# One ScalarE Silu in place of Tanh, Identity and a VectorE join in the feed-forward stage of a transformer layer

## The reference, cut to what matters

```
x = layernorm(x + attention(x))
h = layernorm(x) * ln_gamma + ln_beta
y = silu(h @ w1 + fc1_bias)            # 256 -> 1024, silu(t) = t * sigmoid(t)
z = y @ w2 + fc2_bias                  # 1024 -> 256
x = layernorm(x + (x + 0.5 * z))
```

## Time and profile before

| | |
|---|---|
| median of three runs | 4122.21 us |
| profiled execution | 4118.34 us, span 4116.5 us |
| granted TensorE clock, mean | 0.974 of full speed |
| TensorE busy | 3901.7 us (95%) |
| VectorE busy | 3559.5 us (86%) |
| ScalarE busy | 2781.8 us (68%) |
| GpSimd busy | 867.2 us (21%) |
| last stage | from about 3065 us to the end |

### The profile page before, as it was taken

How to read it: one execution, slowest core, us unless ns; L and a number is a source line. 1 busy time by engine, 2 the same in 40 slices (tenths; PEclk the granted TensorE clock), 3 DMA queues, 4 the chain that set the end, 5 groups by cost and what they waited for, 6 DMA issues and landing times. The chain is left out here.

```text
span 4116.5 us, 78021 instructions
## 1 busy us (share of the span) xinstructions
PE 3901.7 (95%) x22952; PEld 2042.5 (50%) x22952; DVE 3559.5 (86%) x4373; ACT 2781.8 (68%) x5283; POOL 867.2 (21%) x535
## 2 busy tenths in 40 slices
PE   7988999999999999999999999999968999899898
PEld 5653333333333333333333333333326887778777
DVE  6658999999999999999999999999948999989996
ACT  3436888888888888888888888888744444444444
POOL 5430000000000000000000000000006777767774
PEclk9998999999999999999999999999978999999999
DMA  7992113004113211311411311221121122122210
GB/s 253 338 307 55 33 34 82 30 29 82 32 32 64 52 30 41 71 32 32 83 32 32 64 45 32 53 62 32 36 65 53 62 67 76 62 61 68 75 61 26
DMA packets 217885, 286.39 MB, mean 70 GB/s; under 512 B 25521, under 2 KB 127921, under 8 KB 217778
## 3 DMA queue, kind: packets, MB, share of 16 engines
q1 hardware_dynamic: 217778, 285.33, 24.7%
HBM read 165.69 MB, written 118.49 MB: 69 GB/s over the span
## 5 line engine op out<-in xcount | busy, mean ns | idle before, releaser
L685 DVE TENSOR_REDUCE half_max<-first_ps 128x2 f32<-128x1024 f32 x2048 | 2413.4, 1221 | 262.6 <-PE first_ps L579 258.6
L660 ACT ACTIVATE probs<-score_ps 128x512 f32<-128x512 f32 x4096 | 2114.8, 603 | 561.5 <-PE score_ps L604 561.5
L604 PE MATMUL score_ps<-q_s,k_s 49*128 49x512 f32 x4096 | 1435.1, 474 | 22.8 <-DMA q_s<-max_row 7.0
L604 PEld LDWEIGHTS score_ps<-q_s,k_s 49*128 49x128 f32 x4096 | 569.6, 184 | 1279.5 <-ACT probs L660 1179.3
L614 PE MATMUL pv_ps<-probs,v_s 128*32 128x512 f32 x8192 | 1094.2, 606 | 0.0
L579 PE MATMUL first_ps<-k_s,q_s 48*128 48x512 f32 x4096 | 905.3, 421 | 20.9 <-PEq L639 12.9
L1052 POOL TENSOR_TENSOR num<-num,rden 128x1024 f32<-128x1024 f32 x32 | 86.7, 2710 | 2775.5 <-DMA rden<-rden_d 2775.5
L902 ACT ACTIVATE tanh<-fc_ps,b_half 128x512 f32<-128x512 f32 x256 | 175.2, 685 | 472.6 <-PE fc_ps L857 467.9
L579 PEld LDWEIGHTS first_ps<-k_s,q_s 48*128 48x128 f32 x4096 | 402.5, 187 | 73.6 <-DVE half_max L685 18.6
L1033 POOL TENSOR_TENSOR a_lo<-act_f,a_hi 128x512 fp32r<-128x512 f32 x256 | 375.3, 1466 | 173.2 <-DVE a_hi L985 173.2
L980 DVE SCALAR_TENSOR_TENSOR act_f<-tanh,y 128x512 f32<-128x512 f32 x256 | 298.6, 1166 | 56.3 <-ACT y L904 55.8
(11 more groups left out here) (85 smaller groups left out, 2754.7 us busy)
## 6 DMA issues: line engine op xcount, KB each, us to landing
q_s<-q_hi_d SPq DMA_DIRECT2D x512, 64.0 KB, 2.1
o_d<-o_sb SPq DMA_DIRECT2D x128, 256.0 KB, 2.0
x_in<-x_in SPq DMA_DIRECT2D x32, 512.0 KB, 4.9
q_hi_d<-q_hi SPq DMA_DIRECT2D x32, 512.0 KB, 3.1
q_lo_d<-q_lo SPq DMA_DIRECT2D x32, 512.0 KB, 3.9
v_d<-v_f SPq DMA_DIRECT2D x32, 512.0 KB, 4.3
k_s<-k_hi_d SPq DMA_DIRECT2D x128, 128.0 KB, 4.2
v_s<-v_d SPq DMA_DIRECT2D x32, 512.0 KB, 6.5
```

What stands on the lines that cost most here:

```text
L604: pe.matmul(bank(s, u)[:, :], k_s[g][at, a, t * P:(t + 1) * P], q_s[g][at, a, :], start=True, stop=True).then_inc(scored, 1)
L660: nc.scalar.activation(probs[s % 2][:, u, :], bank(s, u)[:, :], ACT.Exp).then_inc(exped, 1)
L685: dve.reduce_max(half_max[g % 2][:, :, a * TT + t, keys], first_ps[keys][:, :, :], AX.X)\
```

## The change

Silu is made by one ScalarE instruction from PSUM, with the bias, straight into `act_f`. The two intermediate pairs of buffers `tanh` and `y`, the VectorE join, the semaphore `pre_up` and the halved bias `b1_half` go; `act_f` has eight buffers (`RING = FC`); ScalarE takes over the wait on the low part, now eight tiles back; and `w2` is scaled by 0.5 instead of 0.25.

```diff
-                nc.scalar.activation(w2_s[:, k:k + FH, :], w2_s[:, k:k + FH, :], ACT.Copy, scale=0.25)\
+                nc.scalar.activation(w2_s[:, k:k + FH, :], w2_s[:, k:k + FH, :], ACT.Copy, scale=0.5)\
...
-            dve.tensor_tensor(b1[:, :], b1_ps[:, :], col[:, B1_C:B1_C + FC], ALU.add).then_inc(filled, 1)
-            dve.wait_ge(filled, 1)
-            dve.tensor_scalar(b1_half[:, :], b1[:, :], 0.5, None, ALU.mult)
+            dve.tensor_tensor(b1[:, :], b1_ps[:, :], col[:, B1_C:B1_C + FC], ALU.add)
...
-        RING = 4
+        RING = FC
...
-        tanh, y = [sb(f"tanh{i}", [P, QB]) for i in two], [sb(f"y{i}", [P, QB]) for i in two]
...
-                pe.wait_ge(pre_up, FC * 2 * n + 2 * f + 2)
+                pe.wait_ge(act_up, FC * n + f + 1)
...
-            def before_silu(n, f):
-                act.wait_ge(act_up, FC * n + f + 1)
+            def silu(n, f):
+                act.wait_ge(alo_up, FC * n + f + 1)
                 act.wait_ge(fc1_mm, 1 + FC * n + f + 1)
-                nc.scalar.activation(tanh[f % 2][:, :], fc1_ps[f % 2][:, :], ACT.Tanh,
-                                     bias=b1_half[:, f:f + 1], scale=0.5).then_inc(pre_up, 1)
-                nc.scalar.activation(y[f % 2][:, :], fc1_ps[f % 2][:, :], ACT.Identity,
-                                     bias=b1[:, f:f + 1]).then_inc(pre_up, 1)
+                nc.scalar.activation(act_f[f % RING][:, :], fc1_ps[f % 2][:, :], ACT.Silu,
+                                     bias=b1[:, f:f + 1]).then_inc(act_up, 1)
...
-            def activate(n, j, f):
-
-                dve.wait_ge(alo_up, FC * n + f + 1)
-                dve.wait_ge(pre_up, FC * 2 * n + 2 * f + 2 + 4)
-                dve.scalar_tensor_tensor(out=act_f[f % RING][:, :], in0=tanh[f % 2][:, :], scalar=1.0,
-                                         in1=y[f % 2][:, :], op0=ALU.add, op1=ALU.mult).then_inc(act_up, 1)
+            def upper(n, j, f):
+
                 if f == 0:
                     dve.wait_ge(fc2_mm, 2 * n + 1)
                 dve.wait_ge(act_up, FC * n + f + 3)
                 dve.tensor_copy(a_hi[j][:, f, :], act_f[f % RING][:, :]).then_inc(ahi_up, 1)
```

More of the change, by code:

```diff
@@ L74, in build_layer @@
         w2_hi, w2_lo = keep("w2_hi", [P, FC, C], F32R), keep("w2_lo", [P, FC, C], F32R)
-        b1, b1_half = keep("b1", [P, FC]), keep("b1_half", [P, FC])
+        b1 = keep("b1", [P, FC])
         ob = keep("ob", [P, TT, C])
@@ L127, in setup @@
 def setup(nc, e):
-    col, ident, wo, b1, b1_half, ob, b2_half = (e[k] for k in ("col", "ident", "wo", "b1", "b1_half", "ob", "b2_half"))
+    col, ident, wo, b1, ob, b2_half = (e[k] for k in ("col", "ident", "wo", "b1", "ob", "b2_half"))
     qb_scaled, minus_half = e["qb_scaled"], e["minus_half"]
@@ L141, in setup @@
             sem(n) for n in ("small_loaded", "w1_loaded", "w2_loaded", "wo_loaded", "wqkv_loaded"))
-        consts, masked, vb_up, bias_up, filled = (sem(n) for n in ("consts", "masked", "vb_up", "bias_up", "filled"))
+        consts, masked, vb_up, bias_up = (sem(n) for n in ("consts", "masked", "vb_up", "bias_up"))
         w1_up, w2_up, scaled, full_up, hi_up, b1_done = (
@@ L722, in finish @@
         e[k] for k in ("x_blk", "out_blk", "o_d", "rden_d", "all_dens", "all_rdens", "ident", "wo"))
-    w1_hi, w1_lo, w2_hi, w2_lo, b1, b1_half, ob, b2_half, minus_half = (
-        e[k] for k in ("w1_hi", "w1_lo", "w2_hi", "w2_lo", "b1", "b1_half", "ob", "b2_half", "minus_half"))
+    w1_hi, w1_lo, w2_hi, w2_lo, b1, ob, b2_half, minus_half = (
+        e[k] for k in ("w1_hi", "w1_lo", "w2_hi", "w2_lo", "b1", "ob", "b2_half", "minus_half"))
     ctx, sb, ps, sem = stage(nc)
@@ L759, in finish @@
             sem(n) for n in ("x1_up", "x1b_up", "hid_up", "ht_mm", "hhi_up", "hlo_up"))
-        fc1_mm, pre_up, act_up, ahi_up, alo_up, fc2_mm, r3_up, y_up = (
-            sem(n) for n in ("fc1_mm", "pre_up", "act_up", "ahi_up", "alo_up", "fc2_mm", "r3_up", "y_up"))
+        fc1_mm, act_up, ahi_up, alo_up, fc2_mm, r3_up, y_up = (
+            sem(n) for n in ("fc1_mm", "act_up", "ahi_up", "alo_up", "fc2_mm", "r3_up", "y_up"))
         sp_begun = sem("sp_begun3")
@@ L916, in body @@
                     if r.has(0):
-                        before_silu(n, f)
+                        silu(n, f)
                     if f == 2 and r.has(-2):
@@ L925, in body @@
                     hidden_hi(n + 1)
-            act.sem_inc(pre_up, 4)
             act.sem_inc(act_up, 2)
@@ L988, in body @@
                 n = r.n
-                tile = (lambda f: activate(n, r.buf(0), f)) if r.has(0) else (lambda f: None)
+                tile = (lambda f: upper(n, r.buf(0), f)) if r.has(0) else (lambda f: None)
                 if r.has(-2):
```

## The result

The changed kernel takes 3978.76 us (median of four runs, 3973.41 to 3983.98), the one before 4122.03 us: ratio 0.9656, 95% interval 0.964 to 0.9672, or 143 us less. Forecast were 3991 us in a range from 3968 to 4050.

A forecast was written before the change was run, and what follows sets the result against it. VectorE, its joins and casts waiting for GpSimd, bounded the kernel; afterwards TensorE would: 31 x 26.74 = 829, plus 12 edges, plus 6 misses, 847 against 973.1 us; with -1.4 at the end, 4118.3 - 127.4 = 3991 us, range 3968 to 4050.

The forecast's parts named there:

- TensorE's work in a round: Last stage: 4.76 + 21.98 = 26.74 us at full clock, forecast to set each of the 31 rounds.
- The wait for `h_lo`: TensorE's 84.3 us in 32 places waiting for VectorE, forecast to go, with the clock keeping its upper level.
- the 1.0 us of slack: End of a round: `h_lo` forecast done 1.0 us before TensorE wants it, level if the cast is held throughout.
- Silu at 0.69 us: ScalarE's Silu per tile, priced like Tanh or Identity at 0.69 us, with 0 and 1.37 us as ends.
- rival C: ScalarE switches function tables six times a round: 4016 us at a low price, 4173 us at twice it; chance 0.08.
- GpSimd's loop: From `project_out` over statistics, roots and low parts to `a_lo` 7: 28.7 us falling to 26.3, range 25.9 to 27.8.
- The loop's edge: VectorE's pause before `r` every fourth round, about 1.5 us in each of 8 places: 12 us, from 0 to 20.
- small misses: Between equal chains in the 31 rounds: 0.2 us a round, 6 us added.
- The end of the stage: Two instructions of 0.69 us leave the last tile's path: -1.4 us.
- A: GpSimd's chain sets the round at 27.8 us with contention as now: 4018 us; chance 0.20.
- B: `h_lo` is late anyway, gap of 1 to 2 us, clock still falling, rounds 29.5 us: 4059 us; chance 0.10.

The follow-up runs named there:

- e9: Changed kernel with VectorE's last reciprocal moved later, its SyncE store put later and the Silu table loaded in ScalarE's idle time: 3969.22 us, ratio 0.9631.
- e12: e9 with the high part made by a second Silu on ScalarE instead of VectorE's cast: 3966.16 us, ratio 0.9628.
- e3: Kernel before with one Sigmoid per tile on ScalarE and a VectorE join reading one input from PSUM, four buffers: 4014.36 us, ratio 0.9734.
- e4: Kernel before with Silu in one ScalarE instruction but a join-like VectorE instruction kept, four buffers: 4128.91 us, ratio 1.0008.
- e8: Changed kernel with one more VectorE instruction per tile, statistics of `act_f` that nobody reads: 3997.8 us, ratio 0.9684.
- e2: Kernel before with VectorE making `h_lo` before join and cast 6 instead of after them: 4121.0 us, ratio 0.9989.
- e5: Changed kernel without one of the three products of `fc2`, so less work for TensorE: 3968.91 us, ratio 0.962.
- e10: e5 also without GpSimd's `x_res` add (output projection's bias missing): 3907.05 us, ratio 0.9475.
- e6: Changed kernel with every Silu done twice, the first into a buffer that nobody reads: 3985.58 us, ratio 0.9662.
- e7: Kernel before with eight `act_f` buffers instead of four, nothing else: 4119.88 us, ratio 0.9997.
- e11: Kernel before without GpSimd's `x_res` add (output projection's bias missing): 4051.55 us, ratio 0.983.

## Why the prediction was right, point by point

- TensorE's work in a round: 26.74 us forecast, 26.84 us measured; 0.1 us is the spacing of 512-column matmuls, 0.234 us in this kernel and 0.231 in the one before. What makes that difference is open; with it gone (e9, e12) a round takes 26.65 us.
- The wait for `h_lo` and the slow clock go: as forecast, with the 1.0 us of slack that was worked out.
- Silu at 0.69 us: measured 0.685. One table load in the stage, so rival C did not occur. It did not fall into ScalarE's idle time but into the first tile.
- The cause, VectorE's joins with their waits for GpSimd: shown by e3 and e4, with e8 for the part of their length. But the text put it at `h_lo`, and e2 shows that this was only where it surfaced.
- GpSimd's loop: forecast as closing through `project_out` at 26.3 us. By that path it takes 26.84 - 1.4 = 25.4 us. The loop that counts closes, by the rows of e5, through the casts, at 26.87 us, as long as TensorE's work to within 0.03 us. So "TensorE sets the round" is half of it: two limits coincide, and taking work from TensorE alone gains next to nothing. That the forecast still had TensorE ahead is in part luck: the loop it priced is not the one that counts. Nor has this loop a fixed length, or e9's rounds with the same casts could not take 26.65 us. What gives way is the cast of tile 7. In the changed kernel `x_b` starts a little later in each round beside TensorE, and this cast, which waits for its end, grows: 1.88, 1.94, 2.01 us and so on. Then it gets ahead of `x_b` and takes 0.41 us, and the next round begins again at 1.88:

```profile
3399.50 2.52 DVE L975 CAST a_hi<-act_f 128x512 fp32r<-128x512 f32 x1
...
3426.37 0.41 DVE L975 CAST a_hi<-act_f 128x512 fp32r<-128x512 f32 x1
```

  In e9 this comes every third or fourth round, in the changed kernel every tenth; in e5 the cast stays at 2.63 to 2.65 us, all but once until the last rounds.
- The loop's edge, +12 us, is the term that failed. The text took 8 places; before, the trace has 6, with 10.8 us in all:

```profile
DVE r L967 <- issue: 10.8, 6, 1.9
```

  In the changed kernel VectorE's residual starts there without a pause, as here (the cast before it waits for GpSimd, 2.35 us):

```profile
3587.39 2.35 DVE L975 CAST a_hi<-act_f 128x512 fp32r<-128x512 f32 x1
3589.66 1.27 DVE L961 TENSOR_TENSOR r<-fc_ps,x_b 128x512 f32<-128x512 f32 x2
```

  The 1.85 us of the earlier trace rows have no counterpart there. A cast that waits covers part of the pause: in e3 the casts before the edge take 1.9 us instead of 1.4, and the pause is 0.5 us shorter. But that is not all of it: in e10 these casts take 1.4 us, as in the kernel before, and there is no pause. Why it went is open. The 6 us for small misses did not come either. So 832.6 us stand against 847.
- The end of the stage: 48.55 us before (4067.95 to the end), 44.8 after, -3.7 us against -1.4.
- The start: the first `fc1` comes 10.0 us later in the profiled execution, although its distance to the attention stage's last store is 46.4 us against 46.9. The attention stage, whose code is the same, ended later. The sum -140.5 - 3.7 + 10.0 is the difference of the two spans, 134.3 us. The medians differ by 143 us.

Rivals A and B did not occur. Near A is the loop of e5, level with TensorE's work; against B the slack held: Silus 0.6 us later cost 0.2 us a round (e6), 5.5 us more on VectorE 0.7 us (e8).

## What to carry to other kernels

Count an instruction that shares something with another engine by what it takes in its place in the profile (1166 ns), not alone (680 ns), and what it makes the other wait; here about 3.3 of the 4.55 us a round came with the waiting and 0.7 to 1.2 with the length. The instruction before which an engine waits is where a loop shows and need not be what closes it: move the waiting step, and if the wait turns up elsewhere at the same period, look for the loop. And when one limit is met, take work from it in a trial to see how far the next one is; here there was next to no distance.

## What was not expected of the hardware

- The edge of the hardware loop costs VectorE a pause in some of these kernels and nothing in others. Before, and in e2, e4, e7 and e11, which keep the join of two SBUF inputs, it is 1.8 to 2.1 us in each of six places, in e3, with the PSUM join, 1.3 to 1.6 us. In the changed kernel and all that are made from it there is none, also where VectorE is busy 580 of 600 us with as many instructions in a round as before (e8). So neither the number of instructions nor VectorE's busy share decides it alone; what does is open.
- The order of two engines at what they share can flip from one round to the next: in the changed kernel the cast of tile 7 takes up to 2.66 us behind `x_b` and 0.41 us ahead of it, and after each flip `x_b` starts 0.8 us earlier beside the cast, where it had come later and later before.
- The clock at the end of the attention stage differs between executions of the same code. In the stretch from 3024 to 3060 us the granted clock was 0.71 before and 0.51 after, and the stage's last store came at 3047.9 and 3058.4 us; over the profiles of all kernels here it lies between 3044.0 and 3058.4 us. A difference of 10 us in a profile of this kernel says nothing unless that stage is set aside. The row of the changed kernel for that stretch (columns as in the table of stretches above):

```profile
3024.00:3060.00 36.00, 31.01 (x101) 7.77 (x101) 3.98 (x2) 17.58 (x34) 0.00 (x0) 0.51 0.04 16
```
